# Router and capacity mixture of the second layer: two looped stages become one unrolled stage

## The reference

```
p = softmax(x @ gate_w.T)                      # 8 experts
two best experts of each token; per sequence and expert count the tokens; keep the first 40 (capacity)
dispatch[e, b, c, :] = the token that sits in slot c of expert e in sequence b
h   = silu(dispatch @ w1[e]) * (dispatch @ w3[e])      # 128 -> 448
out = h @ w2[e]                                        # 448 -> 128
final[b, s, :] = sum over (e, c) of out[e, b, c, :] * p[b, s, e] where token s sits in that slot
y = layernorm(x + final)                               # no gain, no bias
```

## Time and profile before

| | |
|---|---|
| median of 3 runs | 2250.47 us |
| the profiled execution | 2251.52 us, its span 2249.7 us |
| PE busy | 1986.1 us (88%) |
| DVE busy | 1406.2 us (63%) |
| ACT busy | 1287.7 us (57%) |
| POOL busy | 453.3 us (20%) |
| router, from the end of the stage before | 1871.7 to 1912 us |
| mixture | 1912 to 2249.7 us |

### The profile page before, as it was taken

The page is one execution under the profiler, slowest core; times in us unless marked ns, Lnnn a source line. Parts: engine busy times, 40 slices in busy tenths (PEclk is TensorE's granted clock), DMA queues, the critical chain, the costliest instruction groups (busy, mean ns, idle before and its releaser), DMA issues.

```text
span 2249.7 us, 47403 instructions
## 1 busy us (share of the span) xinstructions
PE 1986.1 (88%) x16072; PEld 1496.5 (67%) x16072; DVE 1406.2 (63%) x3578; ACT 1287.7 (57%) x4657; POOL 453.3 (20%) x784
## 2 busy tenths in 40 slices
PE   3639999999999999998699999799996775989987
PEld 1228888888888888886476767566654554556555
DVE  4776777777777777775466565577764773342442
ACT  2216776667777776665244444599996892333332
POOL 1110111111111111111212120244442331110110
PEclk8769999999999999998799999799997995999999
DMA  7000000000000000001000000100000000000000
GB/s 219 11 0 2 2 1 2 2 2 2 1 2 2 2 2 2 2 2 51 16 1 1 1 1 1 34 2 2 2 2 24 13 5 1 1 10 0 9 9 9
DMA packets 27232, 25.40 MB, mean 11 GB/s; under 512 B 3068, under 2 KB 23556, under 8 KB 27016
## 3 DMA queue, kind: packets, MB, share of 16 engines
q1 hardware_dynamic: 27016, 22.62, 3.6%
HBM read 20.52 MB, written 2.10 MB: 10 GB/s over the span
## 4 chain that ended last, share of the span: by engine, by line
issue 62%; PE 14%; POOL 8%; ACT 7%; POOLq 6%; DVE 1%; DMA 1%; DVEq 0%; ACTq 0%; SPq 0%
PE bank L1962 5%; ACT work L1487 5%; POOL work L949 2%; PE bank L1972 2%; PE bank L1422 2%; ACT work L1495 1%; POOLq L952 1%; POOL H L953 1%; POOL work L937 1%; POOL work L1042 1%; PE bank L1989 1%; PE bank L1431 1%; POOLq L1833 1%; POOLq L1831 1%; POOL work L1823 1%
## 5 line engine op out<-in xcount | busy, mean ns | idle before, releaser
L817 ACT ACTIVATE work<-bank,work 128x128 f32<-128x128 f32 x1024 | 364.6, 405 | 223.9 <-DVE work L870 223.9
L697 PE MATMUL bank<-work,wbig 128*128 128x128 f32 x2048 | 262.0, 276 | 0.6 <-ACT work L858 0.5
L817 ACT ACTIVATION_READ_ACCUMULATOR work<-bank,work 128x1 f32 x1024 | 250.5, 245 | 0.0
L697 PEld LDWEIGHTS bank<-work,wbig 128*128 128x128 f32 x2048 | 245.7, 193 | 1.2 <-ACT work L858 0.8
L877 DVE TENSOR_TENSOR work<-work 128x512 f32<-128x512 f32 x256 | 177.3, 693 | 19.5 <-issue 0.5
L870 DVE TENSOR_REDUCE work<-bank 128x4 f32<-128x512 f32 x256 | 159.0, 684 | 33.7 <-PE bank L736 33.7
L1487 ACT ACTIVATE work<-bank,work 128x128 f32<-128x128 f32 x512 | 176.1, 347 | 4.3 <-DVE work L1523 4.3
L832 ACT ACTIVATE work<-bank 128x512 f32<-128x512 f32 x256 | 170.5, 667 | 13.3 <-PE bank L710 13.3
L710 PE MATMUL bank<-ident,work 128*128 128x128 f32 x1024 | 156.3, 275 | 3.1 <-DVE work L877 3.1
L1962 PE MATMUL bank<-work,wbig 128*112 128x320 f32 x512 | 151.0, 439 | 8.5 <-DVE work L2060 5.3
L1176 ACT ACTIVATE work<-bank,col_b 128x512 f32<-128x512 f32 x128 | 87.2, 687 | 104.0 <-PE bank L1104 104.0
(11 more groups left out here) (283 smaller groups left out, 4098.3 us busy)
## 6 DMA issues: line engine op xcount, KB each, us to landing
wbig<-in_moe_w SPq DMA_DIRECT2D x2, 1792.0 KB, 9.8
work<-in_mask_l SPq DMA_DIRECT2D x8, 256.0 KB, 2.9
out<-X SPq DMA_DIRECT2D x4, 512.0 KB, 3.2
H<-in_moe_w SPq DMA_DIRECT2D x1, 1792.0 KB, 9.4
wff<-in_moe_w SPq DMA_DIRECT2D x1, 1024.0 KB
wbig<-in_sa_wq SPq DMA_DIRECT2D x1, 512.0 KB, 3.7
wbig<-in_sa_wk SPq DMA_DIRECT2D x1, 512.0 KB, 4.6
wbig<-in_sa_wv SPq DMA_DIRECT2D x1, 512.0 KB, 5.6
```

The lines of the kernel that those rows point to most:

```text
L697: last = nc.tensor.matmul(o[:, j * T:(j + 1) * T], w[:, t * 128:(t + 1) * 128], src, start=True, stop=True)
L817: last = nc.scalar.activation(at_probs[:, g, h, :], bank[g][:, h * T:(h + 1) * T], ACT.Exp, bias=at_nmax[:, g, h:h + 1], accum_out=at_den[ ...
```

## The change

The two stages become one, `tail1_*`, with no loops and no `end_stage` between.

- Router: PE transposes straight out of X into banks 0 to 3 in turn, two groups ahead of the logits; ACT copies the even groups and DVE the odd ones, into a buffer for all 8. The logits of all groups go to bank 4 and DVE reads them there. POOL's fetch and ACT's copy of the logits are gone, as is DVE's last copy (line 1917).
- Tiles: the 448 hidden units of an expert are three tiles of 128 (two up matmuls each) and one mixed tile in which one matmul with 128 stationary columns holds 64 units of w1 and 64 of w3. So an expert has 7 up matmuls instead of 8 and 4 down matmuls as before. The 7 results take turns in banks 0 to 4; `overwritten` says which tile's product must be over. For the fourth down matmul, w2 and `m1_h` have 64 partitions of zeros (two DVE memsets, one POOL memset in the stage before).
- Order: the down matmuls of the expert before come after the second tile. Sequences 0 to 7 are dispatched before the first tile, through the one bank 6. Everything else that concerns sequences sits between tiles, 32 slots an iteration: in the first iteration its own spreads of the combine matrix (slots 2 to 9); in the others the turn and gather of the 8 sequences before (slots 2 to 10); in the first three the dispatch and spread of the next 8 (slots 14 to 29). Dispatch and turn share bank 6, spread and gather bank 7. The turns and gathers of the last 8 come after the last tile, over three and two banks.
- Norm and store go by 4 sequences instead of 8. The weights come by 8 DMAs instead of 3. For the first 8 sequences DVE builds the one-hots twice.

```diff
         wbig = sb("wbig", [128, 8 * INNER])
         w_att = [[wbig[:, (4 * a + k) * INNER:(4 * a + k + 1) * INNER] for k in range(4)] for a in range(2)]
-        w1_l1 = wbig[:, 0:E1 * F1].rearrange("p (e f) -> p e f", e=E1)
-        w3_l1 = wbig[:, E1 * F1:2 * E1 * F1].rearrange("p (e f) -> p e f", e=E1)
-        w2_l1 = H[:].rearrange("p b d -> p (b d)")[0:FP1, 0:E1 * FT1 * D].rearrange("p (e t m) -> p e t m", e=E1, t=FT1)
+        w13_l1 = wbig[:, 0:2 * E1 * F1].rearrange("p (e f) -> p e f", e=E1)
...
+        m1_disp = [r.take(E1, NB1, CAP) for _ in range(2)]
+        m1_combT = [r.take(NB1, 3, T), None]
+        m1_s = [r.take(SLOTS) for _ in range(3)]
+        m1_h = [r.take(FT1, SLOTS) for _ in range(2)]
+        m1_out = [r.take(3, D) for _ in range(2)]
+        m1_outT = [wff[:, k * NB1 * EC:(k + 1) * NB1 * EC].rearrange("p (b e c) -> p b e c", b=NB1, e=E1)
+                   for k in range(2)]
+        g1_xT = [wff[:, c * W:(c + 1) * W] for c in range(NIT)]
+        TURN_AT, SPREAD_AT = 2, 14
+        LAST = NIT1 - 1
...
+        def spots(k, t):
+            u = 7 * k + 2 * t
+            return bank[u % 5], bank[(u + 1) % 5]
+        def overwritten(k, t):
+            u = 7 * k + 2 * t + (1 if t < PAIRS else 0) - 5
+            return tile_at(u // 7, u % 7 // 2) + 1 if u >= 0 else 0
...
+        def tail1_pe(pe):
+            def tokens(c):
+                need(pe, (g1.xT_act, g1.xT_dve)[c % 2], (c - 4) // 2 + 1)
                 for b in range(NB):
+                    last = nc.tensor.transpose(bank[c % 4][:, b * T:(b + 1) * T], X[:, NB * c + b, :], ident[:])
+                last.then_inc(g1.xT, 1)
+            def logits(c):
+                pe.wait_ge((g1.xT_act, g1.xT_dve)[c % 2], c // 2 + 1)
                 for b in range(NB):
+                    k = NB * c + b
+                    last = nc.tensor.matmul(bank[4][:, k * E1:(k + 1) * E1], g1_xT[c][:, b * T:(b + 1) * T],
                                             gate1[:, :], start=True, stop=True)
                 last.then_inc(g1.logits, 1)
+            def dispatch(b):
+                pe.wait_ge(m1.onehot, hot_in(b) + 1)
+                need(pe, m1.six_read, into(b))
+                nc.tensor.matmul(bank[6][:, 0:EC], X[:, b, :], m1_hot[b % 2].rearrange("p e c -> p (e c)"),
+                                 start=True, stop=True).then_inc(m1.disp, 1)
+            def spread_(b):
+                pe.wait_ge(m1.combine, b + 1)
+                need(pe, m1.seven_read, into(b))
+                for c, (c0, m) in enumerate(CHUNKS):
+                    last = nc.tensor.transpose(bank[7][0:m, c * T:(c + 1) * T], m1_comb[b % 2][:, c0:c0 + m], ident[:])
+                last.then_inc(m1.combT, 1)
+            def up(n, e, t):
+                k = n * E1 + e
+                if e == 0 and t == 0:
+                    pe.wait_ge(m1.six_read, into(NB1 * n + NB1 - 1) + 1)
+                need(pe, m1.hidden, overwritten(k, t))
+                x = m1_disp[n % 2][:, e, :, :].rearrange("p b c -> p (b c)")
+                first, second = spots(k, t)
+                if t < PAIRS:
+                    f = 128 * t
+                    nc.tensor.matmul(first[:, 0:SLOTS], w13_l1[:, e, f:f + 128], x, start=True, stop=True)
+                    f = F1 + REST + 128 * t
+                    nc.tensor.matmul(second[:, 0:SLOTS], w13_l1[:, e, f:f + 128], x, start=True, stop=True)\
+                        .then_inc(m1.up, 1)
+                else:
+                    f = 128 * PAIRS
+                    nc.tensor.matmul(first[:, 0:SLOTS], w13_l1[:, e, f:f + 2 * REST], x, start=True, stop=True)\
+                        .then_inc(m1.up, 1)
+            def down(k):
+                pe.wait_ge(m1.hidden, tile_at(k, FT1 - 1) + 1)
+                need(pe, m1.down_sb, k)
+                for t in range(FT1):
+                    last = nc.tensor.matmul(bank[5][:, 0:SLOTS], w2_l1[:, k % E1, t, :], m1_h[k % 2][:, t, :],
+                                            start=(t == 0), stop=(t == FT1 - 1))
+                last.then_inc(m1.down, 1)
+            def turn(b, o, behind):
+                pe.wait_ge(m1.down_sb, E1 * (b // NB1 + 1))
+                need(pe, m1.six_read, outof(b) - behind)
...
+            def gather(b, o, behind):
+                pe.wait_ge(m1.six_read, outof(b) + 1)
+                need(pe, m1.seven_read, outof(b) - behind)
...
+            for c in range(NIT):
+                tokens(c)
+                if c >= 2:
+                    logits(c - 2)
+            logits(NIT - 2)
+            logits(NIT - 1)
...
+            for b in range(NB1):
+                dispatch(b)
+            pe.wait_ge(m1.zeroed, 1)
+            for n in range(NIT1):
+                for e in range(E1):
+                    for t in range(FT1):
+                        at_ = tile_at(e, t)
+                        up(n, e, t)
+                        b = at_ - TURN_AT
+                        if n == 0 and 0 <= b < NB1:
+                            spread_(b)
+                        if n >= 1 and 0 <= b < NB1:
+                            turn(NB1 * (n - 1) + b, bank[6], 0)
+                        if n >= 1 and 0 <= b - 1 < NB1:
+                            gather(NB1 * (n - 1) + b - 1, bank[7], 0)
+                        b, other = (at_ - SPREAD_AT) // 2, (at_ - SPREAD_AT) % 2
+                        if n < LAST and 0 <= b < NB1:
+                            if other:
+                                spread_(NB1 * (n + 1) + b)
+                            else:
+                                dispatch(NB1 * (n + 1) + b)
+                        if t == 1 and n * E1 + e >= 1:
+                            down(n * E1 + e - 1)
+            down(NIT1 * E1 - 1)
+            for b in range(NB1 + 1):
+                if b < NB1:
+                    turn(NB1 * LAST + b, (bank[6], bank[0], bank[1])[b % 3], 2)
+                if b >= 1:
+                    gather(NB1 * LAST + b - 1, (bank[7], bank[2])[(b - 1) % 2], 1)
...
+            def silu(k, t):
+                u = tile_at(k, t)
+                act.wait_ge(m1.up, u + 1)
+                need(act, m1.hidden, u - 2)
+                o, i = (0, 128) if t < PAIRS else (128 - REST, REST)
+                nc.scalar.activation(m1_s[u % 3][o:128, :], spots(k, t)[0][0:i, 0:SLOTS], ACT.Silu).then_inc(m1.silu, 1)
...
+                nc.vector.tensor_reduce(g1_max, raw, AX.X, ALU.max)
+                dve.drain()
+                nc.vector.tensor_tensor(g1_shifted, raw, spread(g1_max), ALU.subtract).then_inc(g1.shifted, 1)
...
+            def spread_(b):
+                dve.wait_ge(m1.combT, b + 1)
+                o, m = m1_combT[(b // NB1) % 2], CHUNKS[2][1]
+                nc.vector.tensor_copy(o[:, b % NB1, 0:2, :].rearrange("p c t -> p (c t)"), bank[7][:, 0:2 * T])
+                nc.vector.tensor_copy(o[0:m, b % NB1, 2, :], bank[7][0:m, 2 * T:3 * T]).then_inc(m1.seven_read, 1)
...
+            def hidden(k, t):
+                u = tile_at(k, t)
+                dve.wait_ge(m1.silu, u + 1)
+                if t == 0:
+                    need(dve, m1.down, k - 1)
+                first, second = spots(k, t)
+                p, gate = (0, second) if t < PAIRS else (128 - REST, first)
+                nc.vector.tensor_tensor(m1_h[k % 2][p:128, t, :], m1_s[u % 3][p:128, :], gate[p:128, 0:SLOTS], ALU.mult)\
+                    .then_inc(m1.hidden, 1)
...
+            for b in range(NB1):
+                need(dve, m1.disp, b - 1)
+                onehot(b)
+            for n in range(NIT1):
+                for e in range(E1):
+                    for t in range(FT1):
+                        at_ = tile_at(e, t)
+                        b = at_
+                        if n == 0 and 0 <= b < NB1:
+                            if b < 2:
+                                dve.wait_ge(m1.disp, NB1 - 1 + b)
+                            else:
+                                dve.wait_ge(m1.combine, b - 1)
+                            onehot(b)
+                        hidden(n * E1 + e, t)
+                        b = at_ - TURN_AT
+                        if n == 0 and 0 <= b < NB1:
+                            spread_(b)
+                        if n >= 1 and 0 <= b - 1 < NB1:
+                            residual(NB1 * (n - 1) + b - 1, bank[7])
+                        if n >= 1 and b - 1 in (NB, NB1):
+                            stats_(2 * (n - 1) + (b - 1) // NB1)
+                        if n >= 1 and b - 3 in (NB, NB1):
+                            normal(2 * (n - 1) + (b - 3) // NB1)
+                        b, other = (at_ - SPREAD_AT) // 2, (at_ - SPREAD_AT) % 2
+                        if n < LAST and 0 <= b < NB1 and other:
+                            spread_(NB1 * (n + 1) + b)
+                        b, other = (at_ + 2 - SPREAD_AT) // 2, (at_ + 2 - SPREAD_AT) % 2
+                        if n < LAST and 0 <= b < NB1 and not other:
+                            b += NB1 * (n + 1)
```

(56 more changed lines are left out.)

414 lines of the change are left out of this document (162 added, 252 removed).

## The result

The changed kernel takes 2189.22 us (4 runs, 2189.10 to 2189.26) against 2250.62 beside it; the ratio is 0.9728, 95% interval 0.9711 to 0.9745. Forecast were 2186.0 and a range of 2171 to 2212. The profiled execution took 2189.22 us, its span 2187.4: 62.3 less than the profiled one before.

What follows compares the result with a forecast made beforehand. PE was taken as the bound in the experts' part, 52.3 of 53.7 us busy. Terms 19.4 + 10.4 + 13.8 + 249.0 + 20.5 = 313.1 against 378.0, 64.9 less: 2186 us, range 2171 to 2212.

Steps and rivals of the forecast that it cites:

- router: Start of the rewritten stage: eight groups at 2.38 us without waits, at half clock, plus the last matmul and wake-up; 19.4 us.
- choice: Choice of experts after the router: the same chain, 10.3 us, plus a drain of 0.1; 10.4 us.
- first eight dispatches: Before the first tile, through one bank: 1.96 us each at half clock, 1.33 at full, half of each, plus first one-hot; 13.8.
- body: Experts' part: tiles 189.2, pieces in slots 51.8, shape changes 3.4, first-iteration losses 3.3, last product's wait 1.3; 249.0 us.
- end: After the last down matmul: last turns and gathers at 1.34 a sequence, last norm 3.90 instead of 6.60; 20.5 us.
- Rivals B: Pieces in slots cost more than their shares: PE loses 0.3 us in each of 83 slots; 2219 us, chance 0.17.
- C: Slower than before: each of 83 slots pays an uncovered 1.33 us round trip, 2296 us; loses from 0.78 a slot; chance 0.03.
- Rival A: Gapless router lifts the clock early: router 13.3 us instead of 19.0, dispatches 2.6 us less; total 2178 us, chance 0.16.
- The upper end of my bounds: First eight dispatches all at half clock: 15.7 us, before the 0.6 for the first one-hot with its hand-over.
- the 1.0 that I had set aside for changing shape: Slots between tiles: 1.0 us in all for PE changing between instruction shapes at dispatches and spreads.
- 3.3 by hand: First iteration's slots, stepped through with measured durations: PE loses 3.3 us to DVE's one-hots, products and copies, with spreads.
- At nothing: Items costed at zero: POOL's memset in the stage before (POOL idles 8.28 us there), extra DMAs, fewer semaphores, instruction loading.

Runs made afterwards that it cites:

- first experiment: Changed kernel with the mixed tile's matmul issued twice into the same bank, so 8 + 4 matmuls an expert; 2204.59 us, ratio 0.9793 to the kernel before.
- second: Changed kernel with dispatches, spreads, turns and gathers taken out of the slots into blocks around the experts' tiles; 2225.27 us, ratio 0.9883 to the kernel before.
- fourth experiment: Changed kernel with eight added 512-column matmuls on PE during the choice of experts, results unread; 2186.28 us, ratio 0.9711 to the kernel before.
- third experiment: Changed kernel with the first eight dispatches alternating between banks 6 and 5; 2179.21 us, ratio 0.9681 to the kernel before.
- eleventh run: Changed kernel with the router's 32 transposes done as ordinary matmuls against the identity; 2186.23 us, ratio 0.9709 to the kernel before.
- tenth run: Changed kernel with POOL's memset moved one stage later, from the second layer's self-attention to its cross-attention; 2192.40 us.

## Why the prediction was right, and where its terms were off

| Term | forecast | measured | |
|---|---|---|---|
| router | 19.4 | 20.1 | 2.45 a group, not 2.38; 0.50 as said |
| choice | 10.4 | 10.1 | |
| first eight dispatches | 13.8 | 16.7 | half clock for all eight |
| body | 249.0 | 254.2 | below |
| end | 20.5 | 19.2 | last norm 3.90 as said; what follows it 2.8, was 3.9 |
| stage | 313.1 | 320.3 | |
| ahead of the stage | 0 | -4.65 | 2.0 by POOL's memset, 1.6 open, 1.04 scatter |

The mechanism held: PE's own instruction time bounds the experts' part (first experiment), and the pieces are hidden in slots at PE's price (second). Rivals B and C needed waits of 0.3 and 0.78 a slot; the slots showed about 3 us in all, and the wait in today's third tile went, as argued. Rival A failed on the transposes, as the earlier trace rows had suggested.

*The step that was mis-sized most* is the clock behind the router. For the first dispatches I took half the eight at each level, since "PE is busy for a bit over half the time". It was, for 11.28 of 16.74, and the clock stayed down for all eight; even one that was up fell there (fourth experiment). The upper end of my bounds, 15.7, plus 0.6 was nearly right: 2.9 us. For the same reason the first tiles ran at half until 1919.35, another 2.6, which the forecast's range had and its sum had not.

*The pieces.* Dispatch cost 0.54 as said. A spread cost 0.33, not 0.28 (32 x 0.05 = 1.6), turn and gather 1.385, where 1.345 was taken (1.0); the 1.0 that I had set aside for changing shape pays part of it. Behind the mixed tile the gather's first hand-over shows, 0.34 in each of three iterations: the copy of one turn is not quite hidden in the shortest slot. The first iteration lost 3.0 to spreads and one-hots, 3.3 by hand. The weight load of the last down matmuls waited 1.55, not 1.3. So: 32 x 5.92 + 24 x 0.54 + 32 x 0.33 + 24 x 1.385 + 2.6 + 3.0 + 1.0 + 1.5 = 254.3.

*At nothing: POOL's memset.* I looked only at POOL's idle time. POOL had room, but the memset held up DVE, and DVE held up PE by 0.74; by the clock behind it the stage then ended 2.0 earlier. That my total came within 3.2 us is in part luck: an error of 7.2 in the stage stood against 4.65 outside it, of which I had foreseen nothing. The stage alone was forecast at a gain of 64.9 and gained 57.65.

*What was left on the table.* The forecast counted the round trip through bank 6 eight times over and did not ask whether another bank was free. Bank 5 was, and it is worth 10 us (third experiment).

## What to carry to other kernels

Short dependent pieces cost an engine its own instruction time when something independent stands between their halves, and the round trip when they stand together (here 0.87 against 1.40 us for a dispatch with a spread). Price both ways, and look for a stretch where pieces still stand together, as the first eight dispatches do here. There a second bank gave back both the wait (8.2 us) and the clock of what follows (2.4 us). Work put on an idle engine is free only if no other engine slows down beside it: look at the neighbours' durations in the rows, not only at its own idle time. And before an experiment that shifts something is read, look whether the shift arrived at the engine that it was meant for.

## What the runs showed of the hardware that was not expected

- 20.01 of 20.09 us of transposes and 8-column matmuls leave the clock at 0.50; with ordinary matmuls in the transposes' place the router's windows show 0.92 at 1872 to 1874 us and 1.00 from there to the router's end. The Trainium skill, "TensorE: Matmul & The Clock Gate", Part 4, has transposes not count as busy; the eleventh run agrees.
- Waits of 0.62 us between dispatches, with ACT's copy behind each, let a clock that was up at 1898 us fall to half by 1902 (fourth run); the same dispatches through two banks lifted it from half to 1.00 between 1904 and 1906 (third run).
- A POOL memset of 0.94 us stretched DVE copies of 0.18 to 1.00 and PE's wait by 0.74; with it the clock stayed up, and the work at 1460 us came 2.0 us earlier than in the four kernels without it (tenth run). PE's wait before the clock held or fell was the same in both, 1.32 and 1.31.
